# A Swin block on one core: image 0's reciprocal deviation by square root, reciprocal and a Newton step, and image 1's transposes placed behind the first one-hot matmuls

## What is computed

```python
y = layernorm(x) * g1 + b1            # (x - mean) * rsqrt(var + 1e-5)
y = roll(y, (-2, -2)); qkv = windows(y) @ qkv_w + qkv_b
attn = softmax(q * SCALE @ k.T + bias[rel_pos] + mask)
x = x + roll_back(windows_back(attn @ v @ proj_w + proj_b))
z = layernorm(x) * g2 + b2
return x + gelu(z @ fc1_w + fc1_b) @ fc2_w + fc2_b
```

## Time and profile before

| | us |
|---|---|
| median of 3 runs | 231.94 |
| the runs | 231.94, 233.01, 230.03 |
| the profiled execution, its own time | 230.33 |
| its span, first to last instruction | 228.5 |
| PE busy | 208.5 (91%) |
| DVE busy | 165.0 (72%) |
| ACT busy | 148.6 (65%) |
| GpSimd busy | 128.2 (56%) |

### The profile page before, as it was taken

How to read it: one execution, slowest core, us unless ns; L and a number is a source line. 1 busy time by engine, 2 the same in 40 slices (tenths; PEclk the granted TensorE clock), 3 DMA queues, 4 the chain that set the end, 5 groups by cost and what they waited for, 6 DMA issues and landing times.

```text
span 228.5 us, 8108 instructions
## 1 busy us (share of the span) xinstructions
PE 208.5 (91%) x3342; PEld 118.3 (52%) x3342; DVE 165.0 (72%) x253; ACT 148.6 (65%) x217; POOL 128.2 (56%) x116
## 2 busy tenths in 40 slices
PE   0779966899999999999999999999999999979884
PEld 0734523556565556655655566566556555443221
DVE  3896756666877777878787877786766757866874
ACT  7475167656676677677757775867555555577883
POOL 8765669272447956794778397632742092160740
PEclk9997999999999999999999999999999999999999
DMA  6826346654524532452255045405520000000233
GB/s 196 244 74 178 108 131 195 177 170 150 165 72 148 164 102 96 144 163 80 95 166 163 11 136 166 122 10 164 179 83 4 6 6 4 1 3 0 105 127 138
DMA packets 24284, 25.41 MB, mean 111 GB/s; under 512 B 3556, under 2 KB 21732, under 8 KB 24164
## 3 DMA queue, kind: packets, MB, share of 16 engines
q1 hardware_dynamic: 23496, 24.16, 34.0%
q10 hardware_dynamic: 752, 0.74, 1.2%
HBM read 16.24 MB, written 8.39 MB: 108 GB/s over the span
## 4 chain that ended last, share of the span: by engine, by line
issue 39%; POOL 36%; PE 10%; ACT 6%; DVE 3%; DMA 2%; SPq 1%; POOLq 1%; ACTq 0%; DVEq 0%
POOL rstd L376 17%; POOL X L406 4%; POOL parts L394 4%; POOL yn L386 3%; POOL X L411 3%; POOL xc L368 3%; PE ps L962 3%; DMA slots<-parts 2%; ACT q_rows L740 1%; POOL mean L356 1%; ACT k_rows L740 1%; POOL var L362 1%; PE pq L962 1%; PE pav L992 1%; ACT k_rows L745 1%
## 5 line engine op out<-in xcount | busy, mean ns | idle before, releaser
L524 DVE TENSOR_REDUCE negm<-ps 128x8 f32<-128x1024 f32 x64 | 78.2, 1223 | 32.7 <-PE ps L898 32.5
L735 ACT ACTIVATE prob<-ps 128x1024 f32<-128x1024 f32 x64 | 65.5, 1023 | 39.7 <-PE ps L925 39.6
L376 POOL TENSOR_TENSOR rstd<-var,neghalf 128x16 f32<-128x16 f32 x16 | 47.4, 2962 | 17.3 <-DVE var L489 16.4
L912 PE MATMUL ps<-rel_j,id_b 96*32 96x512 bf16 x512 | 39.5, 381 | 3.1 <-ACT prob L735 2.9
L945 PE MATMUL pav<-prob,va 128*32 128x128 f32 x1024 | 41.1, 279 | 0.0
L945 PEld LDWEIGHTS pav<-prob,va 128*32 128x32 f32 x1024 | 24.1, 109 | 12.5 <-issue 5.0
L876 PE MATMUL ps<-rel_i,ident_b 64*64 64x512 bf16 x256 | 26.7, 407 | 0.2 <-DVE negm L524 0.2
L925 PE MATMUL ps<-q_rows,k_rows 64*128 64x128 bf16 x512 | 25.4, 219 | 0.4 <-DMA q_rows<-m_mid 0.4
L898 PE MATMUL ps<-k_rows,q_rows 64*128 64x128 bf16 x512 | 25.2, 219 | 0.0
L394 POOL TENSOR_TENSOR parts<-rest,parts 128x512 bf16<-128x512 f32 x15 | 17.3, 1158 | 13.6 <-ACT parts L719 13.6
L925 PEld LDWEIGHTS ps<-q_rows,k_rows 64*128 64x128 bf16 x512 | 14.4, 94 | 15.5 <-issue 14.6
(11 more groups left out here) (134 smaller groups left out, 333.8 us busy)
## 6 DMA issues: line engine op xcount, KB each, us to landing
slots<-parts SPq DMA_DIRECT2D x21, 256.0 KB, 2.4
q_rows<-slots SPq DMA_DIRECT2D x42, 128.0 KB
k_rows<-slots SPq DMA_DIRECT2D x40, 128.0 KB
X<-x_tok SPq DMA_DIRECT2D x8, 256.0 KB, 4.0
y_tok<-res SPq DMA_DIRECT2D x7, 256.0 KB, 2.0
q_rows<-m_hi SPq DMA_DIRECT2D x32, 4.0 KB
q_rows<-m_mid SPq DMA_DIRECT2D x32, 4.0 KB
bias_parts<-rel_parts SPq DMA_DIRECT2D x3, 128.0 KB
```

The lines of the kernel that those rows point to most:

```text
L376: pool.tensor_tensor(rstd[:, i, :], var[:, i, :], neghalf[:], ALU.pow).then_inc(rstd_done[i], 1)
L524: dve.tensor_reduce(dst, first_home(j)[:].rearrange("p (a u n) -> p a u n", u=2, n=TOK), AX.X, ALU.max, negate=True).then_inc(max_done, 1)
L735: act.activation(prob[:, j % NPROB, :], ps2[:], ACT.Exp).then_inc(exp_done, 1)
L912: pe.matmul(ps2[32 * c:32 * (c + 1), 512 * e:512 * (e + 1)], id3_b[0:96, :], rel_j[0:96, c, e].unsqueeze(2).to_broadcast([96, 2, 2, TOK]), ...
```

## The change

Image 0's reciprocal deviation is no longer made by GpSimd's power. ACT takes the square root of the variance, DVE the reciprocal of that, and one Newton step (three DVE operations) refines it. ACT gets two tiny activations: a square root as its first, and an exponential ahead of the MID gathers. Means of image 1 are finished on DVE only behind image 0's scale. Image 1's square moves behind `copy_yT(0)` on ACT; its variances and its scale move later on DVE, and its transposes on PE go behind the first select and the projection of v's bias (line 1030). `copy_yT(1)` goes behind the first q_rows copy. On DVE the LOW part of `rel_j` moves from ahead of image 1's scale to behind the first k_rows copy, and image 2's means behind the second one. On GpSimd image 1's low part of image 0 stands ahead of image 2's `center`, and there is one power less. SP's order stays.

```diff
@@ gpsimd
-            power(first_norm(0))
             power(first_norm(1))
-            pool.wait_ge(yn_done[1], 1)
+            low_part(0, 1)
             center(first_norm(2), 2)
-            low_part(0, 1)
@@ vector
             variances(first_norm(0))
             dve.wait_ge(d_x[1], 16)
-            means(first_norm(1), 1)
+            sums(first_norm(1), 1)
+            dve.wait_ge(dev_done, 1)
+            dve.reciprocal(guess[:], dev[:]).then_inc(guess_done, 1)
+            dve.wait_ge(guess_done, 1)
+            dve.scalar_tensor_tensor(err[:], guess[:], -0.5, guess[:], ALU.mult, ALU.mult).then_inc(err_done, 1)
+            dve.wait_ge(err_done, 1)
+            dve.tensor_tensor(dev[:], err[:], var[:, 0, :], ALU.mult).then_inc(err_done, 1)
+            dve.wait_ge(err_done, 2)
+            dve.scalar_tensor_tensor(rstd[:, 0, :], dev[:], 1.5, guess[:], ALU.add, ALU.mult).then_inc(rstd_done[0], 1)
+            scale(first_norm(0))
+            dve.wait_ge(sum_done[1], 1)
+            dve.tensor_scalar(mean[:, 1, :], ssum[:, 1, :], 1.0 / C, None, ALU.mult).then_inc(mean_done[1], 1)
             center(first_norm(1), 1)
...
-            variances(first_norm(1))
-            scale(first_norm(0))
             dve.wait_ge(relj_hi, 1)
             dve.tensor_tensor(rel_rest, rel_raw, rel_parts[:, HIGH, :], ALU.subtract).then_inc(relj_rest, 1)
+            variances(first_norm(1))
...
             dve.tensor_scalar(w1[:], P("w1"), P("g2"), None, ALU.mult).then_inc(w_ready, 1)
-            dve.wait_ge(d_x[2], 16)
-            means(first_norm(2), 2)
-            dve.wait_ge(relj_mid, 1)
-            dve.tensor_tensor(rel_parts[:, LOW, :], rel_rest, rel_parts[:, MID, :], ALU.subtract).then_inc(relj_low, 1)
-            scale(first_norm(1))
...
             dve.tensor_tensor(f_bias[:], Q0[:, 128:129], P("fc1b"), ALU.add).then_inc(b_ready, 1)
+            scale(first_norm(1))
             dve.wait_ge(pb_ps, 1)
             dve.tensor_tensor(pb[:], Q0[:, 256:256 + C], P("pb"), ALU.add).then_inc(pb_ready, 1)
             dve.wait_ge(sel_done, 1)
             dve.tensor_copy(k_rows[:, 0, 0:1024], ps2[:]).then_inc(k_first, 1)
+            dve.wait_ge(relj_mid, 1)
+            dve.tensor_tensor(rel_parts[:, LOW, :], rel_rest, rel_parts[:, MID, :], ALU.subtract).then_inc(relj_low, 1)
             dve.wait_ge(sel_done, 2)
             dve.tensor_copy(k_rows[:, 0, 1024:1536], pch[:]).then_inc(k_first, 1)
+            dve.wait_ge(d_x[2], 16)
+            means(first_norm(2), 2)
@@ scalar
             act.wait_ge(zero_ready, 1)
+            act.activation(tiny[:], zero[:], ACT.Sqrt).then_inc(zero_ready, 1)
...
-            square(first_norm(1))
+            act.wait_ge(var_done[0], 1)
+            act.activation(dev[:], var[:, 0, :], ACT.Sqrt).then_inc(dev_done, 1)
...
             copy_yT(0, Q0)
+            square(first_norm(1))
...
-            copy_yT(1, Q1)
             middle_part(0, 1)
             act.wait_ge(sel_done, 1)
             act.activation(q_rows[:, 0, 0:1024], ps1[:], ACT.Copy).then_inc(q_first, 1)
+            copy_yT(1, Q1)
...
             square(first_norm(2))
+            act.wait_ge(zero_ready, 2)
+            act.activation(tiny[:], zero[:], ACT.Exp).then_inc(zero_ready, 1)
@@ tensor
-            transpose_first(1, Q1)
             pe.wait_ge(sel_ready, 8)
             pe.wait_ge(d_aux_first, 16)
             select_rows((0, 1), ((ps1[:, 0:512], ps1[:, 512:1024]), (ps2[:, 0:512], ps2[:, 512:1024])))
             pe.wait_ge(b_ready, 3)
             pe.matmul(Q0[:, 256:256 + C], v_bias[:], P("wpb"), start=True, stop=True).then_inc(pb_ps, 1)
+            transpose_first(1, Q1)
             pe.wait_ge(pb_ready, 1)
```

## The result

The changed kernel took 234.65 us (median of 4 runs, 233.66 to 235.67) against 231.31 for the kernel before (its three runs and one more, 230.03 to 233.01). The medians differ by 3.3 us; the ratio taken from the executions is 1.0189 with a 95% interval of 1.0124 to 1.0253, which would be 4.4 us. So the kernel is slower, by 3.3 to 4.4 us. The forecast was 237.1 in a range of 233.6 to 239.7, 5.2 slower. The profiled execution took 233.66 with a span of 231.9, 3.4 more than the earlier trace rows. The interval reaches over both sides of 2%: the forecast's 0.60 for slower by more than 2% and its 0.38 for less are not decided.

The account below looks back on a forecast made before the run. The prediction took the start-up chain and SP's in-order queue, without slack, to delay the steady loop: 5.3 late at the first exponential + 0.4 - 0.5 = 5.2, so 231.94 + 5.2 = 237.1 us, range 233.6 to 239.7.

Parts of the forecast that it names:

- Part 1: Image 0's reciprocal deviation by square root: scale ends 1.45 us earlier, transposes 0.7 earlier because PE's fillers hold them.
- Part 2: ScalarE's order: high part and remainder of image 0 come 0.6 us earlier; table load hidden, else 1.5 us.
- Part 3: Image 1's transposes behind the first select: second select starts at 19.0 instead of 18.48, by itself 0.5 us slower.
- Part 4: LOW subtraction moved on DVE: third bias transfer at 19.55 instead of 14.03, SP's queue behind it 5.5 us late.
- The slack: Loop's start: ScalarE's middle parts 4.3 us late, 1.7 slack at the exponential, so 4.2 late at PE's former speed.
- The clock at the loop's start: PE idle from about 28 to 33.5 returns at 1.2 GHz: 1.5 us more, first exponential 5.3 late.
- A separate 0.4 for a longer slow stretch: PE staying slow past the first second scores could add up to 1.5 us; 0.4 was taken.
- 0.5 to be won back at 43.45: Second scores waited 0.4 to 0.5 us for the maxima's transfer; SP only 4.2 late there, so 0.5 comes back.
- PE keeps its clock: Rival, chance 0.2: no slow stretch follows PE's idle at the loop's start; 4.2 us late, 236.1.
- The hidden bias transfer: Rival, chance 0.1: bias rows wanted only at 27.97, so the late transfer is hidden; not slower, 231.3 to 232.4.
- extra table loads: Rival, chance 0.05: functions between ScalarE's two square roots need loads of their own, 1.28 us each; 238.3.
- The slow stretch that lasts over the next pairs: Rival, chance 0.2: PE stays at 1.2 GHz over the next pairs; 6.3 us late, 238.2.

Follow-up runs that it names:

- transposes_late_only: Kernel before with only image 1's transposes moved behind the first select and v's bias, and their copy behind the first q_rows copy; ratio 1.0146.
- after_fill_low_back: Changed kernel with ten filler matmuls in PE's gaps and the LOW subtraction back in its old place; median 232.71 us, ratio 1.0109 to the kernel before.
- order3_fill: order3 with seven filler matmuls in PE's gaps; median 230.42 us, ratio 1.0010 to the kernel before.
- low_late_only: Kernel before with only the LOW subtraction moved behind the first k_rows copy; ratio 1.0130.
- after_fill: Changed kernel with ten filler matmuls in PE's gaps, LOW subtraction still late; median 235.22 us, ratio 1.0188 to the kernel before.
- order3: Changed kernel with LOW subtraction back, image 1's transposes behind the second select, its scale behind the first k_rows copy; 233.64 us, ratio 1.0108 to before.
- low_back: Changed kernel with the LOW subtraction back ahead of the remainders; ratio 1.0142 to the kernel before.

## Why the prediction was right, and where it was not

The forecast's sign and range were right, and the queue that it rested on is the way that decides. One of its parts failed, and that the total still fell into the range is in part luck.

**Part 1** held. The deviation came at 9.08 (9.2 foreseen), the scale ended at 9.8 (9.95), and PE's fillers were the bound: transposes at 10.55 (10.7 to 10.9, from 11.47). The reciprocal took 0.24 (0.2), the square root 0.21 (0.2).

**Part 2** held: high part at 13.24 (13.5), remainder at 14.03 (14.3).

**Part 3** is the step that failed. Its start was nearly right, the second select at 19.89 (19.0); the 0.9 of difference are image 1's scale of 1.64 us and slow transposes. But it was priced at 0.5 us, the delay of the start, with the select as long as before (1.8 us to the first scores). It lasted 3.5 at 1.2 GHz, and the first scores came 3.1 late. transposes_late_only shows that this part makes the kernel 1.5% (about 3.4 us) slower by itself, where the prediction had "0.5 us slower". The prediction looked for the clock only behind the long idle at 28 us, and not at the select. The total came out near because this way and the queue run side by side and the queue was the later one. At the first exponential it was 1.3 less than the forecast's 5.3: 0.5 of that is the shorter landing (Part 4), and PE, whose idle was cut short by the late first scores, came back at full speed. Two errors partly met there.

**A term left out.** The prediction moved image 2's means and priced nothing for it. In the changed kernel itself that is nearly hidden: the square of image 2 started at 26.18, the gathers at 26.98. In after_fill_low_back and order3_fill, with the queue early, it or the copy beside it holds m_hi.

**Part 4** held in mechanism. Its steps were: third transfer 19.85 (19.55), m_hi 29.83 (30.5), bias matmuls 32.72 (33.5). What was too large was the landing of the bias parts: 3.36 us from issue to the gather instead of 4.2, within the bounds given (3.1 to 4.2). With it the queue was 5.0 late and not 5.5. Three of SP's gathers of k also went out within 1.8 us instead of 3.4, so SP was free again only 3.6 later, and the maxima's transfer was only 3.6 late. The table load cost nothing, as Part 2 says, but not for its reason: in the runs with an early queue (after_fill_low_back, order3_fill), where Part 2 would charge 1.5 us, ScalarE issued the gathers during the load.

**The slack** was read rightly: ScalarE's middle parts went 3.5 late (4.3 foreseen), with less slack behind them.

**The clock at the loop's start** was half right. Its start-up rows are weak evidence: the weight loads of 333 ns stand in a stretch (7 to 10 us) whose granted clock reads 1.00. low_late_only bears it out better: after 5.7 us of rest PE's eight bias matmuls took 1.04 us, at a granted clock of 0.50. The foreseen idle of 5.5 us was cut to 1.9 by the late first scores, and still the clock was low from 33.6 to 36.9. In low_late_only and after_fill, where PE did stand idle for 4 to 6 us, the exponential was 5.3 to 5.4 late, the 5.3 of the working. In the changed kernel PE came back at full speed and slowed 0.9 us later; the exponential was 4.0 late. A separate 0.4 for a longer slow stretch can't be told apart there. Of the 0.5 to be won back at 43.45, 0.4 came: the delay went from 4.0 to 3.6.

**The rivals.** The hidden bias transfer and the extra table loads fell: SP's wait of 6.4 us is on the way, and there is one new load (26.83). "PE keeps its clock" was named with 4.2 late; the measured 3.3 to 4.4 is nearest to it in size, but not in mechanism, since the clock did fall, earlier. The slow stretch that lasts over the next pairs (6.3 late) did not come: the clock was back at about 37. The second cause, the slow second select, was no rival of the prediction.

**The range.** The low end does not follow from its own terms: 235.0 less the 1.9 of scatter is 233.1, not 233.6. The measured 234.65 lies within either.

What stays open: the 1% that after_fill_low_back still lacks is only partly accounted for. That image 2's late means hold ScalarE's gathers is read from its trace (1.2 us at m_hi), and no run tests it.

## What to carry to other kernels

Ask of every moved instruction which queue waits for its result in program order, not only which computation does: a 0.7 us subtraction moved by six microseconds held SP, and with it transfers that had been ready for five. Where two ways lead to the same event, undoing either alone shows next to nothing; take each alone in the kernel before and both together in the kernel after, and look again at what names the event then: here a third way came out. And when a reordering opens gaps on PE, price the work behind them at 1.2 GHz as well as at 2.4.

## What the runs showed of the hardware

- PE's clock fell without a long idle. In the changed kernel it was low from 16.5 us, though PE had not rested for more than 0.6 us at a time since 13. With one to three filler matmuls in each of these gaps it held (order3_fill, after_fill). After a rest of 1.9 us it fell in the changed kernel (33.6) and didn't in the kernel before (32.18).
- DVE's scale of 128x512 fp32 took 1.64 us instead of 0.69 where GpSimd ran its own subtraction of the same size beside it (first line below); in order3, with GpSimd idle, it took 0.68 (second). The Trainium skill, "GPSIMD Engine Reference" (Key points), says that the two engines share their SBUF interfaces and contend where a DVE instruction has two SBUF inputs. The trace agrees: the scale has two inputs in SBUF (xc and rstd), and it took 0.95 us more.

```profile
16.30 1.15 POOL L399 TENSOR_TENSOR parts<-rest,parts 128x512 bf16<-128x512 f32 x1
```

```profile
19.85 0.68 DVE L507 TENSOR_TENSOR yn<-xc,rstd 128x512 f32<-128x512 f32 x1
```

- ScalarE's table load (1.28 us) does not hold up its issuing of transfers: in the changed kernel the gathers went out at 26.98, in the middle of the load that began at 26.83, and so ahead of the tiny exponential that stands in front of them in the program (28.12). In low_back four gathers went out one after another from 27.50 to 30.06, with a load from 28.09 to 29.37 among them.
